# Attention with 64-wide heads over 589 keys: GpSimd adds the last 77 keys' exponentials into the sum, and the multiplication by ones makes one round

## What is computed

```python
def _L1_xcond_ref(x, latents, shift, scale, ln1_w, ln1_b, ln2_w, ln2_b, Wq, Wkv, Wo):
    ...
    x = layer_norm(x, ln1_w, ln1_b)
    lat = layer_norm(latents, ln2_w, ln2_b)
    lat = lat * (1.0 + scale[:, None, :]) + shift[:, None, :]
    q = jnp.einsum('bld,ed->ble', lat, Wq)
    ...
    kv_in = jnp.concatenate((x, lat), axis=-2)
    kv = jnp.einsum('bld,ed->ble', kv_in, Wkv)
    k, v = jnp.split(kv, 2, axis=-1)
    ...
    q, k, v = (to_heads(q), to_heads(k), to_heads(v))
    ...
    logits = jnp.einsum('bhqd,bhkd->bhqk', q * attn_scale, k * attn_scale)
    w = jax.nn.softmax(logits.astype(jnp.float32), axis=-1).astype(logits.dtype)
    out = jnp.einsum('bhqk,bhkd->bhqd', w, v)
    ...
    return jnp.einsum('ble,de->bld', out, Wo)
```

## Time and profile before

| | |
|---|---|
| median of 3 runs | 4204.04 us |
| lowest and highest | 4200.7 and 4207.72 us |
| span of the profiled execution | 4207.1 us (its own time is not given apart; the span lies within the runs' spread) |
| instructions | 58174 |
| PE busy | 3747.1 us, 89% |
| DVE busy | 2478.3 us, 59% |
| ACT busy | 2349.6 us, 56% |
| POOL busy | 1323.6 us, 31% |
| mean granted clock of PE | 0.958 of 2.4 GHz |

### The profile page before, as it was taken

How to read it: one execution, slowest core, us unless ns; L and a number is a source line. 1 busy time by engine, 2 the same in 40 slices (tenths; PEclk the granted TensorE clock), 3 DMA queues, 4 the chain that set the end, 5 groups by cost and what they waited for, 6 DMA issues and landing times.

```text
span 4207.1 us, 58174 instructions
## 1 busy us (share of the span) xinstructions
PE 3747.1 (89%) x23065; PEld 1688.2 (40%) x23065; DVE 2478.3 (59%) x4844; ACT 2349.6 (56%) x3290; POOL 1323.6 (31%) x1323
## 2 busy tenths in 40 slices
PE   5699999999999998998896888899998998988886
PEld 4477433333774334334453223333333332333333
DVE  6632444544224434543466977777877777777754
ACT  4543554454335545555421666676777766667783
POOL 5500334334003430352003223434343342342411
PEclk8699999999999999999997999999999999999998
DMA  2000100000000001001121100211111111110100
GB/s 97 1 21 1 46 11 21 11 11 21 27 1 34 21 22 36 6 21 45 32 48 40 39 24 24 60 29 32 57 31 41 42 42 29 42 47 24 37 15 16
DMA packets 113620, 126.84 MB, mean 30 GB/s; under 512 B 34863, under 2 KB 98551, under 8 KB 111428
## 3 DMA queue, kind: packets, MB, share of 16 engines
q1 hardware_dynamic: 113348, 123.12, 9.9%
HBM read 58.00 MB, written 1.45 MB: 14 GB/s over the span
## 4 chain that ended last, share of the span: by engine, by line
PE 63%; DVE 21%; ACT 8%; POOL 5%; issue 2%; DMA 1%; SPq 0%; DVEq 0%; POOLq 0%; ACTq 0%
PE ps L1722 6%; PE ps L1738 6%; PE ps L1642 6%; PE ps L1634 5%; PE ps L1933 5%; DVE c1sm L2626 4%; DVE c0sm L2626 4%; PE ps L1850 3%; PE ps L1919 3%; ACT wB L2165 2%; PE ps L1877 2%; PE ps L1770 2%; PE ps L1663 2%; PE ps L1977 2%; PE ps L1687 1%
## 5 line engine op out<-in xcount | busy, mean ns | idle before, releaser
L2165 ACT ACTIVATE wB<-ps 128x1024 f32<-128x1024 f32 (+1 forms) x767 | 766.9, 1022 | 270.0 <-PE ps L1919 264.2
L2626 DVE TENSOR_REDUCE c1sm<-ps 128x2 f32<-128x1024 f32 x384 | 455.8, 1219 | 118.6 <-PE ps L1877 115.8
L2626 DVE TENSOR_REDUCE c0sm<-ps 128x2 f32<-128x1024 f32 x384 | 452.8, 1218 | 95.6 <-PE ps L1877 93.4
L2463 DVE TENSOR_REDUCE c1sm<-ps 128x2 f32<-128x1024 f32 x128 | 151.3, 1218 | 192.3 <-PE ps L1687 191.5
L2463 DVE TENSOR_REDUCE c0sm<-ps 128x2 f32<-128x1024 f32 x128 | 151.8, 1219 | 172.4 <-PE ps L1687 171.9
L2165 ACT ACTIVATE c0m<-ps 128x1024 f32<-128x1024 f32 (+1 forms) x193 | 197.3, 1022 | 59.3 <-PE ps L1919 57.3
L1933 PE MATMUL ps<-wB,c1m 128*9 128x512 f32 (+1 forms) x1204 | 205.3, 611 | 0.7 <-DVE c1sm L2633 0.3
L1919 PE MATMUL ps<-c0ar 64*128 64x512 bf16 (+1 forms) x864 | 165.2, 387 | 29.5 <-DVE c1sm L2626 12.4
L1919 PE MATMUL ps<-c1ar 64*128 64x512 bf16 (+1 forms) x864 | 165.7, 394 | 26.1 <-DVE c0sm L2626 9.1
L1722 PE MATMUL ps<-c0ar 64*128 64x512 f32 (+1 forms) x640 | 176.7, 629 | 13.6 <-DVE c1sm L2463 5.9
L1722 PE MATMUL ps<-c1ar 64*128 64x512 f32 (+1 forms) x640 | 177.9, 632 | 7.2 <-ACT c1ar L2088 4.6
(11 more groups left out here) (848 smaller groups left out, 8533.4 us busy)
## 6 DMA issues: line engine op xcount, KB each, us to landing
c0ar<-c0m SPq DMA_DIRECT2D x216, 128.0 KB, 2.4
c1ar<-c0m SPq DMA_DIRECT2D x216, 128.0 KB, 2.4
c0m<-rscr SPq DMA_DIRECT2D x96, 128.0 KB, 2.9
c1m<-rscr SPq DMA_DIRECT2D x96, 128.0 KB, 2.9
wA<-in_lay SPq DMA_DIRECT2D x6, 1346.0 KB, 5.7
wA<-in_w SPq DMA_DIRECT2D x1, 4248.0 KB, 22.2
wA<-in_w SPq DMA_DIRECT2D x1, 4104.0 KB, 12.2
wA<-in_w4b SPq DMA_DIRECT2D x1, 2948.0 KB, 10.0
```

The lines of the kernel that those rows point to most:

```text
L2165: e.activation(P.ap[0:n, :, :], u.ap[0:n, :].rearrange("p (a q) -> p a q", a=2), ACT.Exp, scale=S8).then_inc(*A(("P8", n0, s, k), free=[u]))
L2463: e.tensor_reduce(c.sm[:, 2 * (g % 2), 2 * j:2 * j + 2], u.ap.rearrange("p (h k) -> p h k", h=2)[:, :, 0:n], AX, ALU.max, negate=True).the ...
L2626: e.tensor_reduce(c.mneg[:, j, :, s // 4, s % 4], u.ap.rearrange("p (a k) -> p a k", a=2), AX, ALU.max, negate=True).then_inc(*V(free=[u]))
```

## The change

`adds` now runs over all blocks of keys, not over the first four. In stage 2 that makes a fourth operation for each group on POOL, which adds the 77 rows of the last `P` to the first 77 rows of `S`; only that last one now signals that the sum is complete. `evict` hands the last block to `divide` only where it is the sole one, so stage 2's multiplication by ones makes one round of four matmuls for each pair of groups instead of two. The last `P` buffer is given back by POOL's add, not by PE's second round. With four blocks and with one nothing is different.

```diff
             def adds(g):
 
                 (S,), _ = yield Want([], [c.S2])
-                for i in range(1, 4):
+                for i in range(1, nc_):
                     while i not in got[g]:
                         yield
                     _, t = yield Want([("G", 2.5)], after=got[g][i][1])
-                    emit("sa", c, n0, g, i, S, got[g][i - 1][0] if i == 1 else None, got[g][i][0])
+                    emit("sa", c, n0, g, i, S, got[g][i - 1][0] if i == 1 else None, got[g][i][0], chunks[i][0], i == nc_ - 1)
...
-                if nc_ != 4:
+                if nc_ == 1:
                     parts.append((got[g][nc_ - 1][0], chunks[-1][0], nc_ - 1))
...
-                    if nc_ != 4:
+                    if nc_ == 1:
                         used(g + p, nc_ - 1, t[0])
...
-            def sa(c, n0, g, i, S, P0, P):
+            def sa(c, n0, g, i, S, P0, P, n, end):
                 if i == 1:
                     for x in S.clear():
                         w.wait_ge(*x)
                 w.wait_ge(*A.at(("P", n0, g, i)))
                 w.wait_ge(*G.now())
-                e.tensor_tensor(S.ap, P0.ap if P0 else S.ap, P.ap, ALU.add).then_inc(*G(("S", n0, g), free=[P0, P] if P0 else [P]))
+                i = e.tensor_tensor(S.ap[0:n], P0.ap if P0 else S.ap[0:n], P.ap[0:n], ALU.add)
+                i.then_inc(*G(("S", n0, g) if end else None, free=[P0, P] if P0 else [P]))
```

## The result

| | before | changed |
|---|---|---|
| median of 4 runs each | 4202.48 us | 4225.91 us |
| lowest and highest | 4200.7 and 4207.72 | 4222.19 and 4233.41 |
| ratio, 95% interval | | 1.0054 [1.0040, 1.0069] |

The change makes the kernel 23.4 us slower (17 to 29 by the interval). The profiled execution of the changed kernel took 4233.41 us, 7.5 above its median; its span is 4231.5. The forecast was 4205.6, its range 4192 to 4215.

The account below looks back on a forecast made before the run. PE was taken as the bound, busy 89% of the span and nearly full in stage 2. The terms -15.4 + 4 + 1.5 + 10 + 1.5 gave +1.6 us on 4204.0, so 4205.6, range 4192 to 4215.

Parts of the forecast that it names:

- How far the change reaches, and the unchanged rest: Engine orders differ from stage 2's first 77-key block until early stage 4, about 1486 us; the remaining 2,720 us stay unchanged.
- Term 1: Stage 2's multiplication by ones: half its 30.83 us of PE work goes, taken as -15.4 us.
- Term 2: Stage 2's 32 new GpSimd adds, 76 us in all, hide in idle time; waits of the multiplication by ones put at nothing.
- rival c: Stage 2's multiplication by ones waits for the late add, 2.4 us per pair; 4209 to 4240 us, chance 0.04.
- Term 3: Second stream's start in stage 2: a new add delays its double normalization and PE waits; +4 us together.
- Term 4: Stage 2 to stage 3: one step fewer covers the gap before the first stream's transposes; +1.5 us.
- Term 5: Stage 3 to stage 4: both streams end together, PE idles about 10 us before the transposes; net +10, range 6 to 14.
- last stage 3 matmul about 8 us earlier: Sign that the forecast is right: stage 3's last matmul comes about 8 us earlier than before, ahead of the idle gap.
- Term 6: Before projections: more collisions of L2498 with GpSimd adds, between 0 and 5 us in the stage, taken as +1.5.
- (b): GpSimd's new adds block VectorE on PE's path in stage 2, 12.6 us on top; 4218.2 us, chance 0.16.
- (a): The removed matmuls stay gained: stage 4 opens without the long gap or collisions do not come; 4194.6 us, chance 0.18.
- term 5's 3.9: At stage 4's start: four maxima, 4.61 us plus about 1 for the mask, against 1.8 of PE work; 3.9 lost.

Follow-up runs that it names:

- new_work_other_seed_3: The changed kernel with random seed 23 instead of 6349 in stage 3's row of the planner's table; 4194.16 us, 0.9983 of the kernel before.
- seed 6349: The original random seed in stage 3's row of the planner's table, in the kernel before (4202.48 us) and the changed kernel (4225.91 us).
- seed 30: The kernel before with only the random seed in stage 3's row of the planner's table changed from 6349 to 30; 4225.84 us, ratio 1.0054.

## Why the prediction was wrong

The sum was +1.6; the changed part took 24.1 more. By its steps:

- **How far the change reaches, and the unchanged rest.** Right: -2.9 us behind the common matmul, inside the 4 allowed. But with traces of equal order 15.9 us apart there, one pair of traces is weak support.
- **Term 1, -15.4.** Size off: the busy time of the earlier trace rows halves to 17.05, but from L1759 to the next line it is 1.00 instead of 1.86, so 16 x 0.86 = 13.8. Booking it as gained whole was nearly right in the new order, 12.7 by the two traces there. In before's order, from which I argued, 6.4 is gained and the rest comes back: "an instruction off PE is time gained unless PE then waits" was true, and there PE did wait.
- **Term 2, the adds hidden.** Right in size (the 77-row adds take 2.35) and in that no L1759 waits for one; rival c did not occur. But "VectorE stands still while GpSimd adds" was too wide, see below.
- **Term 3, +4.** Right: A is +4.7. Both L2246 groups take 3.15 (first 1.12 before), L1651 waits 2.94 instead of 0.89. Without the adds the new order loses 3.2 less there, in before's order 3.7 less.
- **Term 4, +1.5.** Right: E is +1.7; PE waits 4.20 before L1531.
- **Term 5, +10.** The place and the mechanism were right: 9.65 idle against 9 to 11 forecast, 27.9 us from the last expert matmul (ends at 1285.57) to the first scores. But I ended the account with the second preparation. F is +12.1, and G adds +9.0 in the next 140 us, where the new order puts L2498 and casts under adds and PE drops to its lower clock. **This is the step that failed**: I took the seam for an event of 28 us, and the newly planned order goes on for 200. The sign "last stage 3 matmul about 8 us earlier" was wrong as well: it ends 13.8 earlier (1299.39 to 1285.57), 17.0 counted from each trace's first scores, because before has two preparations and four steps of scores of the first stream ahead of it, which now stand behind; I had not taken that moved work out.
- **Term 6, +1.5.** Failed: C and D are +7.3 (2.6 of it are the new adds, in C; the rest is the order). At the change of batch a PE that was busy 49.63 of 60 us (730 to 790) is busy 43.93. I had looked for waits on the new adds, not for each place where the order differs.
- **Rivals.** (b) named 4218.2 by a mechanism that costs the change 6.9 us in its changed part (6.3 by the medians), 3.2 of it in A, which term 3 had counted; it exists, and before pays for its own adds. (a) was excluded by the measured seam. The time lies inside (c)'s 4209 to 4240, but no L1759 waits for an add. Two sums are a little off without changing anything: term 5's 3.9 is 3.8, and (c) by its own terms is 4210 to 4244.

The Trainium skill (SBUF — State Buffer, SBUF: two separate sides) has GpSimd and those VectorE operations that have two SBUF inputs or run in a two-port mode take an exclusive lock, held for the whole instruction. 3.15 for one add and 5.32 for two agree; so does that none of 256 maxima L2463, which read PSUM, takes over 1.23 us (median 1.22), before, in the changed kernel and in new_work_other_seed_3. The part of the prediction that drew on it was right for L2246 and L2498 and too wide for the maxima, and that each new add might cost 2.37 did not come: 32 adds cost 3.6 us in before's order and 6.9 in the new one.

The deeper error is in weighing. For terms 3 to 6 I read the new order at the four places that I had found, and gave every other place zero or, in term 6, 1.5. The old numbers of the table may suit the old work, though two seeds for each work cannot show it: its waits and slow clock are 80.6 us with seed 6349 and 94.6 with seed 30, and with the same 6349 the new work has 115.3, though 86.8 with seed 23. I read an order that comes out of numbers fitted to another piece of work as a draw, and the places that I did not read should have had a positive price and a wide bound, not zero.

## What to carry to other kernels

If a scheduler decides the order, a change of work is two changes: price the work with the order held fixed, and the order with the work held fixed. Here the work was worth a gain of 0 to 6 us and the order cost 20 to 32. Taking work off the busiest engine is worth less than its time wherever that work covered a wait: 6.4 of 13.8 us in one order, 12.7 in the other. And where two engines block each other, look for the longest operations that a short chain passes through: one wait in GpSimd's queue gave 9 to 18 us by the medians.

## What was not expected of the hardware

- Two GpSimd adds with 0.08 us between them hold a group of four L2246 for 5.32 us instead of 1.11. In that trace each add holds one of the four, which then take 2.38 and 2.50; the other two take 0.35 and 0.34. The pause lets the held one end and the next is held again.
- With less work on PE its clock was lower: 0.79 instead of 1.00 over 8 us around an unchanged wait of 1.85 us, and a lower clock behind that wait in six places of eight, against one of six with the work of before. The Trainium skill (TensorE: Matmul & The Clock Gate, What's actually happening) lets the clock follow how busy the array was lately; the trace agrees, and suggests that removed matmuls can be paid for in this way.
- An add over 77 partitions takes as long as over 128: 2.35 us.
